# Thirty-two bytes: where the buffers of a three-stage kernel lie in on-chip memory

## What is computed

```
h = gelu(grouped_conv(x)) ; h = grouped_conv(h) ; h = layernorm(h + x)      # depthwise, 4 hidden per channel, 5 taps
for i in range(4):                                                          # linear attention, 16 heads of 16
    q, k, v = gelu(h@Wq[i]+bq)+.21, gelu(h@Wk[i]+bk)+.21, h@Wv[i]+bv
    z  = 1 / (q . mean(k) + 1e-6)
    kv = rope(k)^T v / n
    h  = layernorm(rope(q) kv * z + h)
f = gelu(h@W1+b1)@W2+b2 ;  a = layernorm(f + h)                             # first feed-forward, 256 -> 1024 -> 256
x = layernorm(x + a)
W1c, W2c = for each: sum over the top 32 of 64 of softmax weight * (A_k @ B_k)   # composed weights
out = layernorm(x + gelu(x@W1c)@W2c)                                        # second feed-forward
```

## Time and profile before

| | |
|---|---|
| median of 3 runs | 1863.91 us |
| the runs | 1859.66, 1864.61, 1863.91 us |
| the profiled execution | 1859.66 us, its span 1857.9 us |
| granted TensorE clock | 0.998 |
| TensorE matmuls busy | 1832.2 us, 99% |
| VectorE, GpSimd, ScalarE busy | 1416.6, 1011.6, 934.3 us |

### The profile page before, as it was taken

How to read it: one execution, slowest core, us unless ns; L and a number is a source line. 1 busy time by engine, 2 the same in 40 slices (tenths; PEclk the granted TensorE clock), 3 DMA queues, 4 the chain that set the end, 5 groups by cost and what they waited for, 6 DMA issues and landing times.

```text
span 1857.9 us, 50038 instructions
## 1 busy us (share of the span) xinstructions
PE 1832.2 (99%) x21188; PEld 1528.6 (82%) x21188; DVE 1416.6 (76%) x3329; ACT 934.3 (50%) x1741; POOL 1011.6 (54%) x775
## 2 busy tenths in 40 slices
PE   8999999999999999999999999999999999999998
PEld 2334888888888888888887799999999999999998
DVE  3556788888888888888887767777777777777777
ACT  4554667766676667766676653232323232323231
POOL 1455999899999999899996112222222222222221
PEclk9999999999999999999999999999999999999999
DMA  8354120010102110010104940010101010101000
GB/s 291 131 207 184 56 80 17 3 36 2 36 2 104 64 56 11 2 36 2 59 2 134 308 153 32 26 44 26 44 26 44 26 44 26 44 26 42 28 12 24
DMA packets 25249, 115.62 MB, mean 62 GB/s; under 512 B 4481, under 2 KB 5441, under 8 KB 19905
## 3 DMA queue, kind: packets, MB, share of 16 engines
q1 hardware_dynamic: 21104, 89.69, 13.7%
q0 software_dynamic: 1152, 12.58, 1.9%
q10 hardware_dynamic: 2768, 10.15, 1.4%
HBM read 80.95 MB, written 31.46 MB: 61 GB/s over the span
## 4 chain that ended last, share of the span: by engine, by line
PE 96%; DVE 2%; ACT 1%; issue 0%; DMA 0%; POOL 0%; SPq 0%; ACTq 0%; DVEq 0%; POOLq 0%
PE bankC L34 13%; PE bankC L33 13%; PE bankC L32 13%; PE ring L32 7%; PE ring L34 6%; PE ring L33 6%; PE big L917 5%; PE hid_ps L241 4%; PE big L34 3%; PE big L32 3%; PE big L33 3%; PE conv_ps L253 3%; PE ring L854 3%; PE big L834 3%; PE ring L891 2%; PE ring L876 2%
## 5 line engine op out<-in xcount | busy, mean ns | idle before, releaser
L32 PE MATMUL bankC<-down_hi,act_hi 128*128 128x256 f32 x1024 | 291.4, 285 | 0.0
L34 PE MATMUL bankC<-down_hi,act_lo 128*128 128x256 f32 x1024 | 289.6, 283 | 0.0
L33 PE MATMUL bankC<-down_lo,act_hi 128*128 128x256 f32 x1024 | 288.6, 282 | 0.0
L1553 DVE TENSOR_TENSOR act_lo<-gel,act_hi 128x512 fp32r<-128x512 f32 x256 | 210.9, 824 | 8.7
L34 PE MATMUL bankC<-aT_hi,up_lo 128*128 128x512 f32 x512 | 199.7, 390 | 0.0
L33 PE MATMUL bankC<-aT_lo,up_hi 128*128 128x512 f32 x512 | 199.5, 390 | 0.0
L32 PE MATMUL bankC<-aT_hi,up_hi 128*128 128x512 f32 x512 | 199.4, 389 | 0.0
L32 PEld LDWEIGHTS bankC<-down_hi,act_hi 128*128 128x128 f32 x1024 | 193.8, 189 | 1.2
L33 PEld LDWEIGHTS bankC<-down_lo,act_hi 128*128 128x128 f32 x1024 | 193.2, 189 | 1.4
L1507 POOL TENSOR_TENSOR hC<-hC,vecC 128x1024 f32<-128x1024 f32 x16 | 38.5, 2404 | 284.5 <-PE turn L1406 284.5
L34 PEld LDWEIGHTS bankC<-down_hi,act_lo 128*128 128x128 f32 x1024 | 193.2, 189 | 0.0
(11 more groups left out here) (205 smaller groups left out, 5252.1 us busy)
## 6 DMA issues: line engine op xcount, KB each, us to landing
raw_late<-in_AB SPq DMA_DIRECT2D x30, 320.0 KB, 3.9
u<-hA SPq DMA_DIRECT2D x8, 1024.0 KB, 4.6
u_next<-u SPq DMA_DIRECT2D x8, 1024.0 KB, 4.8
hC<-u SPq DMA_DIRECT2D x16, 512.0 KB, 3.9
xC<-in_x SPq DMA_DIRECT2D x16, 512.0 KB, 4.8
out<-w_flat SPq DMA_DIRECT2D x15, 512.0 KB, 2.6
w_flat<-in_AB SPq DMA_DIRECT2D x22, 320.0 KB, 3.7
w_split<-w_parts ACTq DMA_DIRECT2D x4, 1536.0 KB, 5.3
```

Source lines behind the costliest of these rows:

```text
L32: e.matmul(out, wh, xh, start=start, stop=False)
L33: e.matmul(out, wh, xl, start=False, stop=False)
L34: return e.matmul(out, wl, xh, start=False, stop=stop)
L1553: e.tensor_tensor(a_lo[:, fb, :], g, a_hi[:, fb, :].bitcast(F32), ALU.subtract).then_inc(s_act_lo, 1)
```

## The change

Three edits, all of them of places in memory. No instruction is added, removed or moved in any engine's order, and no wait is changed.

```diff
@@ ffn_phase
         b1s, vec = place["b1s"], place["vecC"]
+        minus_half = sb("minus_halfC", [P, TILES])
         x_both, h_both = place["xC"], place["hC"]
         gel = sb("gel", [P, GEL, TOK])
...
         rstd = sb("rstdC", [P, LANES, TILES])
-        minus_half = sb("minus_halfC", [P, TILES])
@@ build
-        under(ctx, [("band1", [P, CP, 2, 4, 32]), ("band2", [P, CP, 4, 2, 32]), ("xs1", [P, CP, T // 2 + 1])], [])
+        under(ctx, [("xs1", [P, CP, T // 2 + 1]), ("band1", [P, CP, 2, 4, 32]), ("band2", [P, CP, 4, 2, 32])], [])
...
-
-        sb("input_end", [P, 16])
+        sb("bands_end", [P, 8])
```

## The result

The changed kernel takes 1877.32 us in the median of 6 runs (1874.20 to 1878.01), the kernel before 1863.90 in 6. Three more runs of the changed kernel, the profiled one among them, lie from 1876.43 to 1879.74. The ratio is 1.0074, with a 95% interval from 1.0061 to 1.0086. It is slower by 13.4 us, just outside the predicted range, whose upper end was 1876.

A forecast was written before the change was run, and what follows sets the result against it. TensorE's step from one matmul's start to the next was taken to bound the kernel; all terms summed to 0 against the profiled execution's 1859.66 us, giving 1863 us for a median, range 1847 to 1876.

The forecast's parts named there:

- The bound: All three stages: how closely TensorE's matmuls follow each other sets the end, for 99% of the time.
- rival D: Attention: GpSimd becomes the bound, its instructions growing by 20%; +79 us, 1942 us; chance 0.04.
- Convolution, bands and `xs`: Convolution operands in new places: taken 0, bounds plus or minus 0.3 us; initial load's wait plus or minus one us.
- `up` against `aT`: Feed-forward up products, 1536 matmuls of 512 columns, operands 32 bytes apart: 0 or +10.1 us, taken 0.
- `w_second`: Attention layers 1 and 3, 16 units, moved 32 bytes against `hT`: taken 0, best -2 us, worst +2.
- `down`: Feed-forward down products against `act`, 3072 matmuls of 256 columns: taken 0, lanes' paces give -2.4 to +2.4 us.
- Rival B: Feed-forward: `up` falls out of step with `aT`, +10.1 us, lane 1 loses its lead, +2.4; 1875.5 us; chance 0.19.
- rival A: Whole kernel: nothing changes, 1863 us, with its terms 1858 to 1868; chance 0.48.
- Rival C: Feed-forward: weight load's reads and stream no longer meet, one step in four 0.01 us shorter; -11.5 us, 1851.5; chance 0.29.

## Why the prediction was wrong

**The bound** was right: TensorE's step from start to start decides, in all three stages, and no other engine became the bound (rival D fell with GpSimd's unchanged 23.7 us).

**Convolution, bands and `xs`** at 0: right, shown by the run that moves them alone (1.0002).

**`up` against `aT`** at 0: this is the step that failed. The term had the bounds 0 and +10.1 us, both from the right rows, and measured +8.9 (the bound counts 6.6 ns for all 48 steps of a product, but the first of them took 229 to 236 ns already before). I took 0 because "an offset of 32 bytes is much nearer to equal than the 128 of `w_second`". That treats the cost as growing with the distance. It does not: 32 costs 233 ns and 128 costs 232, and only 0 gives 227. The rival named this ("any difference undoes it") and gave 1875.5. In the pattern of the earlier trace rows all the equal pairs were fast and the unequal one slow, and no row said that a small distance costs less than a large one; so nothing in the rows spoke for giving the rival the smaller chance.

**`w_second`** at 0: it was 128 away and is 160 away, and cost 1.3 us; inside the bound of 2. That 160 is a little slower than 128 (query products 5.69 for 5.66 to 5.68 us) the prediction had no row for.

**`down`** at 0: 2.7 us in all. Lane 1, whose `act1_lo` lost its equal distance, gives 0.21 and 0.11 us a phase, lane 0 nearly nothing (12.39 and 12.38 for 12.36 and 12.40). Rival B had +2.4 for it by the same argument. The size came out, the argument does not carry far: for 256 columns equal rests are not the best place.

**The range** ended where rival B did, with nothing for `w_second` on top of it; and rival A's own span of 1858 to 1868 is narrower than the sum of the terms that it names. B's 12.5 and the 1.3 are 13.8, against 13.4 measured; 1876 was too low an end for the rival that it was to hold.

**Rival C**, that the steps can be shorter than they are, is real but was not what this change did. Its row was a single step of 0.11; such steps stand between longer ones in lane 0 as well. The runs show a pace of 113 ns that holds for whole down products once both parts of `act` are at the right distance. For 512 columns no run went below 227.

By the rule that TensorE's two read ports are independent (the Trainium skill, TensorE: Matmul & The Clock Gate, Step-by-step: what each phase is for), no distance between the two operands should matter. The runs do not agree: 32 bytes between them take an up product from 10.9 to 11.2 us, whichever of the two is moved. The lines of 16 bytes (the Trainium skill, SBUF — State Buffer, Door 1) do not explain it alone, since every move here is a multiple of 16.

## What to carry to other kernels

Where fp32 matmuls each load their own weights and TensorE is full, write down the addresses of stationary and moving operands modulo 256 before you touch a buffer's size or order, and read the step from start to start for each pair. An insertion of 32 bytes far ahead of the operands can shift one of them and not the other; pad so that 512-column pairs stay equal, and try distances for the shorter ones. Where a trace shows a cost at equal and at unequal, do not interpolate between them.

## What was not expected of the hardware

- The step of a 128x512 fp32 matmul with its own 128x128 weight load is 227 ns when both operands' starts agree modulo 256 bytes and 232 to 233 ns at distances of 32, 128, 192 and 224; absolute alignment to 64 bytes does not matter (both at 32 past: 227).
- The step of a 128x256 one is 113 ns at distances of 192 (hi part) and 64 (lo part), 120 ns at equal ones.
- At the half clock of the changed kernel's composition a 128x256 one steps by 213 ns (12 steps in 2.56 us), which is its 256 columns at 1.2 GHz and nothing over them. The 13 ns over the columns at distance 0 are seen only at the full clock here.
- The same addresses can have two paces; that it is a matter of how a stretch begins is my reading, and not shown. At distance 64 the same up product took 11.01 us after composition and 11.20 after down products. Lane 0's down products, their own buffers unmoved, took 12.36 and 12.40 us after up products of 227 ns and 12.27 to 12.30 after those of 229 to 233 (the runs with `aT` at 32, 64 and 192). A slower up product alone does not do it: lane 1 at the same distances (128, 128) took 12.35 to 12.39 after up products of 232.
- Why 0 is best at 512 columns and 192 with 64 at 256 stays open. No run here separates the reads of the weight load from those of the stream. The two parts of `act` do count each by itself. In lane 1 and network 1 with the hi part at 128, the lo part at 0, 32, 128 and 224 gives 12.23, 12.37, 12.35 to 12.39 and 12.28 us (the last three after slower up products). In lane 0 and network 2 with the lo part at 64, moving the hi part from 64 to 192 takes 12.19 to 11.83. `up` was not tried at 96 and 160.
